# First layer of a four-layer graph kernel: records, score parts and cleared sums made inside the block that computes the scores

## The chip, the cores and the metric

One core of a Trainium2 chip runs the whole program. The metric is device time in microseconds of one execution, the median of several; three executions of the kernel before are shown. The engines are PE (TensorE), DVE (VectorE), ACT (ScalarE), POOL (GpSimd) and SP (SyncE); POOL also issues every indirect DMA of this kernel.

## What is computed

Four residual graph layers over 3125 nodes of 128 features, each behind a layer norm and a relu. Only the first matters here. It is a graph attention of four heads over 50000 edges:

```python
h = jnp.maximum(_layernorm(x, axis=-1), 0.0)
for hd in range(H):                       # H = 4
    h = inputs * W[hd]
    s_src = h @ a[hd, :D]
    s_dst = h @ a[hd, D:]
    e = jnp.exp(jax.nn.leaky_relu(s_src[src] + s_dst[dst], ALPHA))
    rowsum = jax.ops.segment_sum(e, src, num_segments=N)
    agg = jax.ops.segment_sum(e[:, None] * h[dst], src, num_segments=N)
    outs.append(jax.nn.elu(agg / rowsum[:, None]))
x = x + jnp.mean(jnp.stack(outs, axis=-1), axis=-1)
```

## The kernel before

Nodes lie in 25 blocks of 128 (NB = 25, P = 128, D = 128), so a quantity over all nodes and features is a tile of 128 partitions by 3200 elements. The program is a sequence of blocks. Inside a block each engine has its own list of instructions, ordered by semaphores; a block ends when all engines have reached its end, and only then does any engine begin the next one. Nothing is scheduled by a planner: the order of each engine is the order in which the code is written.

`first_layer` (L1854) runs these blocks in a row:

- `layer_norm_once` makes `h`. Beside it POOL runs `put_records` (L911), which writes the sorted edges into a table in HBM, one indirect DMA for 128 edges, and waits after every four until they have landed. 391 such puts are spread over three blocks.
- A short block in which SP loads the weights `w_all`, `w_col` and `a_col`.
- `scores_once` (L440) computes the two scores of each node and head, `s_col` and `d_col`, with exact error terms. ACT scales, PE transposes, ACT copies the transposed strips into `p` and `e`, and DVE sums them. At each head's end DVE raises `added`; ACT's last strip is counted in `taken`, and PE's in `turned`. POOL issues the remaining 289 puts beside it (PUT_BEFORE = 102 to ET = 391) and waits for their landing at its end (`wait_landed`).
- `store_records` (L1482) builds one record of 520 numbers (RECORD) for each node: four heads of 128 products `h * W[k]` and a one behind each, then the four scores `d`. DVE makes the products, one instruction for each head over all 25 node blocks (L1492), ACT copies the scores (L1497), POOL sets the ones (L1502). When all nine are made, POOL scatters the records to `rec_dram`, one indirect DMA for each node block, in the sorted order of the nodes (L1505), and waits for the landing of all 25.
- `spread_parts` (L1510) splits `s_col` into three bf16 parts on DVE (L1526 to L1531), transposes them on PE (L1539), and DVE copies the result to `s_rows` (L1533).
- A block in which POOL clears `y`, the sums, 128 by 12900 numbers (L1885), and the counter `passed` (L1886).
- `end_layer` frees the semaphores behind a barrier, the number of passes is read into registers, and the loop over passes begins. There is one pass here: `sum_neighbours` starts with an iota on POOL (L1618), loads 416 rows of the table, gathers 416 times 128 records (L1628), weighs them and adds them to `y` (L1702).
- `finish_once` divides and applies elu.

Of the kernel before, what the change touches and what calls it, by code (L numbers as in the profile page):

```python
# [10 lines left out]
BF16 = mybir.dt.bfloat16  # L11
# [425 lines left out]
            act.activation(root[:, :], var[:, :], ACT.Sqrt).then_inc(a, 1)  # L437


def scores_once(nc, K, h, w_col, a_col, s_col, d_col, table, listed):  # L440

# [6 lines left out]
    with ExitStack() as stack:  # L448
# [9 lines left out]
        v, turned, taken = c.sem("v"), c.sem("turned"), c.sem("taken")  # L458
        scaled, product_made, error_made, added = c.sem("scaled"), c.sem("product_made"), c.sem("error_made"), c.sem("added")
        units = [("p", 0, 0), ("p", 0, 1), ("e", 0, 0), ("e", 0, 1)]  # L460
        for k in range(1, heads):
# [8 lines left out]
        @block.gpsimd  # L470
        def _(pool):
            put_records(pool, K, table, PUT_BEFORE, ET, listed)
            wait_landed(pool, listed, ET)

        @block.tensor
        def _(pe):
            def turn(n, src, at, count):

                if n >= RING:
                    pe.wait_ge(taken, n - RING + 1)  # L480
                for b in range(count):
                    last = pe.transpose(bank[n % RING][:, b * P:(b + 1) * P], src(at + b), K["ident"][:, :])
                last.then_inc(turned, 1)

            for m in range(STRIPS):
                turn(m, lambda b: h[:, b, :], 4 * m, min(4, NB - 4 * m))
            for n, (kind, k, side) in enumerate(units):
                rows = p_rows[:, k % 2, side, :] if kind == "p" else e_rows[:, side, :]
                if kind == "p":
                    pe.wait_ge(product_made, 2 * k + side + 1)  # L490
                else:
                    pe.wait_ge(error_made, 2 * k + side + 1)
                for m in range(STRIPS):
                    turn(STRIPS * (n + 1) + m, lambda b: rows[:, b * P:(b + 1) * P], 4 * m, min(4, NB - 4 * m))

        @block.scalar
        def _(act):
# [102 lines left out]
ROUND_MAGIC = 12582912.0  # L600
TOP_DEGREE = 4000.0
RECORD = 4 * (D + 1) + 4
KEY_STEP = 4096.0
PARTS3 = 3 * NB

# [873 lines left out]
    step(dve.scalar_tensor_tensor(out, s, 1.0, m, ALU.add, ALU.mult))  # L1479


def store_records(nc, K, h, w_all, d_col, rec_dram):  # L1482
    with ExitStack() as stack:
        c = Ctx(nc, stack, "records")
        rec = c.sb("rec", [P, NB, RECORD])
        stored, made = c.gather_sem("stored"), c.sem("made")
        block = stack.enter_context(nc.Block())

        @block.vector
        def _(dve):  # L1490
            for k in range(4):
                dve.tensor_tensor(rec[:, :, k * (D + 1):k * (D + 1) + D], h, w_all[:, k, 0:D].unsqueeze(1).to_broadcast([P, NB, D]),  # L1492
                                  ALU.mult).then_inc(made, 1)

        @block.scalar
        def _(act):
            act.copy(rec[:, :, 4 * (D + 1):RECORD], d_col[:, :, :].rearrange("p k b -> p b k")).then_inc(made, 1)  # L1497

        @block.gpsimd
        def _(pool):  # L1500
            for k in range(4):
                pool.memset(rec[:, :, k * (D + 1) + D:(k + 1) * (D + 1)], 1.0).then_inc(made, 1)  # L1502
            pool.wait_ge(made, 9)
            for b in range(NB):
                pool.indirect_dma_start(rec_dram, bass.IndirectOffsetOnAxis(ap=K["order"][:, b:b + 1], axis=0),  # L1505
                                        rec[:, b, :], None).then_inc(stored, 16)
            pool.wait_ge(stored, 16 * NB)


def spread_parts(nc, K, stage, own_col, out):  # L1510


# [341 lines left out]
def first_layer(nc, K, table, listed, rec_dram, w_dram, a_dram):  # L1854
# [3 lines left out]
    with ExitStack() as stack:  # L1858
        c = Ctx(nc, stack, "first")
        passed = c.sb("passed", [P, 1])  # L1860
        s_rows = c.sb("s_rows", [PARTS3, heads, P], BF16)
        with ExitStack() as inner:
            ci = Ctx(nc, inner, "scored")
            s_col, d_col = ci.sb("s_col", [P, heads, NB]), ci.sb("d_col", [P, heads, NB])
            h = ci.sb("h", [P, NB, D])[:, :, :]
            w_all, w_col, a_col = ci.sb("w_all", [P, heads, D + 1]), ci.sb("w_col", [P, heads]), ci.sb("a_col", [P, heads, 2])
            layer_norm_once(nc, K, h, "norm0", beside=lambda pool: put_records(pool, K, table, PUT_EARLY, PUT_BEFORE, listed))
            kept = ci.sem("kept")
            with nc.Block() as block:
                @block.sync  # L1870
                def _(sp):
                    sp.dma_start(w_all[:, :, 0:D], broadcast(w_dram)).then_inc(kept, 16)
                    sp.dma_start(w_col[:, :], w_dram.rearrange("h f -> f h"), allow_slow_non_contiguous=True).then_inc(kept, 16)
                    sp.dma_start(a_col[:, :, :], a_dram.rearrange("h (t f) -> f h t", t=2), allow_slow_non_contiguous=True).then_inc(kept, 16)
                    sp.wait_ge(kept, 48)
            scores_once(nc, K, h, w_col, a_col, s_col, d_col, table, listed)
            store_records(nc, K, h, w_all, d_col, rec_dram)
            spread_parts(nc, K, "parts", s_col[:, :, :], s_rows[:, :, :])
        with ExitStack() as inner:
            ci = Ctx(nc, inner, "rounds")  # L1880
            y = ci.sb("y", [P, NB, heads, D + 1])
            with nc.Block() as block:
                @block.gpsimd
                def _(pool):
# [3 lines left out]
            n_passes = nc.values_load(K["passes"][0:1, 0:1], min_val=1, max_val=MOST_PASSES)  # L1888
            with nc.Fori(0, n_passes) as turn:
                with ExitStack() as s:  # L1890
                    sum_neighbours(nc, Ctx(nc, s, "sum"), table, rec_dram, K, s_rows, passed, y, turn)

                end_pass(nc)
            finish_once(nc, K, y)


def sort_edges(nc, K, stack, src, dst, weight, low_dram, row_dram, x_dram, table, listed):
# [1175 lines left out]
```

## Time and profile before

| | |
|---|---|
| median of three runs | 4641.7 us (4637.39 to 4642.4) |
| the profiled execution, its own time | 4645.37 us |
| its span, first to last instruction | 4643.6 us |
| busiest engine over the span | DVE, 2849.6 us, 61% |
| POOL | 1946.6 us, 42% |
| PE | 1605.0 us, 35% |
| mean granted TensorE clock | 0.64 |

No engine is busy throughout: the program is a chain of stages that have different limits, and each block's end holds back whatever comes next. The stage of this change lies between about 1005 and 1084 us of the span. Shares over the whole span say nothing about it; the timeline of that stretch does. In the timeline a row gives the start, the duration, the engine, the line of the code, the operation, and in brackets how long the engine had stood idle and what released it ("SPq L1483" is the sequencer of SP at line 1483, a block's barrier; "issue" is a pause of the engine's own).

### The profile page before, as it was taken

To read this page: it belongs to the slowest core of one execution; us is meant where nothing else is said; L and a number is where in the kernel's file an instruction comes from. 1 tells how busy PE (TensorE), PEld (TensorE's weight loads), DVE (VectorE), ACT (ScalarE), POOL (GpSimd) and SP (SyncE) were. 2 spreads that over 40 slices of the span, in tenths; PEclk is the share of its full clock that TensorE was granted. 3 is DMA by queue.
4 is the path that set the end of the run, shared out by engine and by line. 5 is a ranking of instruction groups with operands and counts; after the bars stand their busy time and mean duration, and the time that the engine had idled before them with its cause. 6 is when DMAs were issued, how large, how long until landed. Compare 5 with 4: busy or idle time off the path is not lost. (4 is left out here: it accounts for less than half of the span.)

```text
span 4643.6 us, 47312 instructions
## 1 busy us (share of the span) xinstructions
PE 1605.0 (35%) x10711; PEld 927.3 (20%) x10711; DVE 2849.6 (61%) x4818; ACT 1636.8 (35%) x4317; POOL 1946.6 (42%) x1847
## 2 busy tenths in 40 slices
PE   3170111100000000003765333142222079899989
PEld 2150111100000000001221111021111069444444
DVE  5866399872677779894554333647878767422131
ACT  1350212101556567203665434124444465010011
POOL 0046555546777730005555555157777550000000
PEclk8585555555555555555676666565555589999999
DMA  3000000005666630001222222168888545777846
GB/s 131 15 20 1 3 1 1 1 21 160 190 185 184 184 94 0 0 0 37 54 63 72 63 63 63 24 192 263 261 256 271 164 134 147 299 239 268 282 156 204
DMA packets 215387, 553.44 MB, mean 119 GB/s; under 512 B 46177, under 2 KB 112411, under 8 KB 214404
## 3 DMA queue, kind: packets, MB, share of 16 engines
q0 software_dynamic: 99984, 272.83, 21.2%
q1 hardware_dynamic: 115188, 278.18, 17.6%
q8 instruction: 82, 1.34, 0.1%
q14 instruction: 133, 1.09, 0.1%
HBM read 485.70 MB, written 65.20 MB: 119 GB/s over the span
## 5 line engine op out<-in xcount | busy, mean ns | idle before, releaser
L2712 PE MATMUL fourth_bank<-fourth_tile,fourth_z 128*128 128x512 f16 (+1 forms) x2800 | 559.8, 361 | 19.8 <-DVEq L2873 10.1
L1192 POOL DMA_INDIRECT blend_got<-rec,blend_slot x416 | 401.0, 964 | 368.6 <-DMA blend_got<-rec,blend_slot 254.8
L917 POOL DMA_INDIRECT table<-edges_record,edges_place x391 | 412.7, 1055 | 294.0 <-DMA table<-edges_record,edges_place 187.8
L2074 POOL DMA_INDIRECT heads_got<-rec,heads_slot x416 | 474.1, 1140 | 134.2 <-issue 126.4
L1628 POOL DMA_INDIRECT sum_got<-rec,sum_slot x416 | 456.5, 1097 | 142.5 <-issue 122.2
L247 PE MATMUL blend_count<-blend_mov,blend_stat 128*128 x980 | 337.9, 440 | 360.6 <-DVE blend_mov L1244 259.4
L1702 DVE TENSOR_TENSOR rounds_y<-rounds_y,sum_got 128x516 f32 x416 | 290.9, 699 | 113.3 <-DVE rounds_y L1702 29.8
L203 PE MATMUL edges_p_key<-kept_ident,edges_key_row 128*128 128x128 f32 x4 | 1.1, 428 | 1019.9 <-DVEq L170 1019.9
L2712 PEld LDWEIGHTS fourth_bank<-fourth_tile,fourth_z 128*128 128x128 f16 x2800 | 261.7, 99 | 311.7 <-issue 15.2
L1244 DVE TENSOR_SCALAR blend_mov<-built_iota_low,built_low 128x800 f16 x490 | 216.2, 442 | 170.8 <-PE blend_count L247 100.5
L2163 DVE TENSOR_TENSOR heads_got<-heads_got,heads_factor 128x390 f32<-128x390 f32 x416 | 232.1, 558 | 108.9 <-issue 99.4
L1232 DVE SCALAR_TENSOR_TENSOR second_sums<-blend_got,blend_weight,second_sums 128x129 f32 x416 | 123.7, 349 | 272.6 <-DMA blend_got<-rec,blend_slot 240.5
L2187 DVE TENSOR_TENSOR third_a_y<-third_a_y,heads_got 128x520 f32 x416 | 287.7, 692 | 1.1 <-DVE third_a_y L2187 0.2
L1719 ACT ACTIVATE sum_got<-sum_got,edges_place 128x129 f32<-128x129 f32 x672 | 197.6, 388 | 239.4 <-DVEq L1679 239.4
L2225 ACT ACTIVATE heads_got<-heads_got,heads_factor 128x65 f32<-128x65 f32 x832 | 217.4, 340 | 89.2 <-DVEq L2157 89.2
L1272 ACT ACTIVATE blend_gap<-built_iota_ten,built_offset 128x128 f32 x490 | 196.8, 402 | 125.3 <-issue 73.0
L247 PEld LDWEIGHTS blend_count<-blend_mov,blend_stat 128*128 x980 | 100.1, 102 | 604.3 <-issue 578.6
L1719 ACT ACTIVATE sum_got<-sum_got,sum_weights 128x129 f32<-128x129 f32 x576 | 169.4, 387 | 121.3 <-DVEq L1679 121.3
L203 PEld LDWEIGHTS edges_p_key<-kept_ident,edges_key_row 128*128 128x128 f32 x4 | 0.7, 216 | 1020.6 <-issue 1020.6
L247 PE MATMUL heads_degrees<-heads_one,heads_flipped 128*128 128x1 f16 x625 | 36.7, 169 | 450.1 <-ACT heads_flipped L2214 362.4
L130 POOL MEMSET edges_src_i<- 128x128 int32 x1 | 0.2, 204 | 417.8 <-POOLq L1081 417.8
L1274 ACT ACTIVATE blend_stat<-blend_gap x490 | 151.5, 309 | 54.3 <-ACT blend_gap L1272 0.8
(666 smaller groups left out, 4401.4 us busy)
## 6 DMA issues: line engine op xcount, KB each, us to landing
fourth_tile<-cs SPq DMA_DIRECT2D x100, 800.0 KB, 4.5
fourth_tile<-ct SPq DMA_DIRECT2D x100, 800.0 KB, 4.3
ct<-blend_cst SPq DMA_DIRECT2D x20, 1000.0 KB
heads_counts<-ct SPq DMA_DIRECT2D x25, 800.0 KB, 8.5
cs<-heads_flipped SPq DMA_DIRECT2D x25, 800.0 KB, 5.3
attend_cnt<-ct SPq DMA_DIRECT2D x50, 256.0 KB, 2.9
sort_low_wide<-low SPq DMA_DIRECT2D x4, 3136.0 KB
attend_cnt<-ct SPq DMA_DIRECT2D x25, 288.0 KB, 3.8
```

Source lines behind the costliest of these rows:

```text
L247: return pe.matmul(out, lhsT, rhs, start=False, stop=True, skip_group_check=True)
L917: pool.indirect_dma_start(table, bass.IndirectOffsetOnAxis(ap=K["place"][0:lanes, t:t + 1], axis=0), K["record"][0:lanes, t, :], None).the ...
L1192: pool.indirect_dma_start(got[:, buf, r, :], None, rec_dram, bass.IndirectOffsetOnAxis(ap=slot[:, t:t + 1], axis=0)).then_inc(gathered[t % ...
L1244: dve.tensor_scalar(at_slot(mov, at), K["iota_low"][:, :], K["low"][:, bass.ds(t, 1)], None, ALU.is_equal).then_inc(mov_ready, 1)
L1628: pool.indirect_dma_start(got[:, t % (HELD * PART), :], None, rec_dram, bass.IndirectOffsetOnAxis(ap=slot[:, t:t + 1], axis=0)).then_inc(g ...
L1702: dve.tensor_tensor(sums, sums, got[:, t % (HELD * PART), 0:heads * F1], ALU.add).then_inc(added, 1)
L1719: last = act.activation(part, part, ACT.Copy, scale=weights[half][:, k, r:r + 1])
L2074: pool.indirect_dma_start(got[:, buf, r, :], None, rec_dram, bass.IndirectOffsetOnAxis(ap=slot[:, t:t + 1], axis=0)).then_inc(gathered[buf ...
L2163: dve.tensor_tensor(part, part, factor[:, buf, r, ON_ACT:heads].unsqueeze(2).to_broadcast([P, heads - ON_ACT, F1]), ALU.mult).then_inc(sca ...
L2187: dve.tensor_tensor(out, out, got[:, buf, r, 0:WIDTH], ALU.add).then_inc(added, 1)
L2225: last = act.activation(part, part, ACT.Copy, scale=factor[:, buf, r, h:h + 1])
L2712: last = pe.matmul(bank[m][:, 0:w], z2[s % 2][:, k, part, :], tile[:, n % RING, at:at + w], start=(k == 0 and part == 0), stop=(k == NB - ...
```

## The change

`store_records` is removed, `spread_parts` is no longer called for the first layer, and the block that clears `y` is gone. Their work moves to the end of each engine's list in `scores_once`, whose end now serves for all of them:

- POOL: behind its last put, it waits for `taken`, sets the ones, clears `passed`, waits for `ones` and `numbered`, and then scatters the 25 node blocks, each behind a wait for its piece of the records. `wait_landed` for the puts comes behind the scatters, followed by the wait for the scatters' own landing.
- DVE: behind the last sums, it makes the records' products in five instructions of five node blocks and all four heads each (RECORD_GROUP = 5), where there were four of one head and all node blocks. `W` is read from PSUM (`w_bank`), where ACT has put it. Then come the bf16 split, the clearing of `y` (before on POOL, now on DVE), and the copy to `s_rows`.
- ACT: copies `W` to PSUM when the last errors are made, and `d_col` into the records when the last sums are made.
- PE: four bf16 transposes at the end of its list.

Memory is shared: the records lie over `p_rows` and `e_rows`, and `p` and `e` lie in `y`, which is now allocated for the whole layer; `w_bank` lies in the PSUM of `part`, the transposes write to the first bank of the ring.

```diff
@@ scores_once
-def scores_once(nc, K, h, w_col, a_col, s_col, d_col, table, listed):
+def scores_once(nc, K, h, w_all, w_col, a_col, s_col, d_col, s_rows, y, passed, table, listed, rec_dram):
...
-        part = c.ps("part", (P, 4 * 512))[:, 0:HALF]
-        p_rows, e_rows = c.sb("p_rows", [P, 2, 2, NP]), c.sb("e_rows", [P, 2, NP])
-        p, e = c.sb("p", [P, 2, NB, D]), c.sb("e", [P, 2, NB, D])
+        part_banks = c.ps("part", (P, 4 * 512))
+        part = part_banks[:, 0:HALF]
+        rows = c.sb("rows", [P, 6 * NP])
+        p_rows = rows[:, 0:4 * NP].rearrange("p (k s n) -> p k s n", k=2, s=2)
+        e_rows = rows[:, 4 * NP:6 * NP].rearrange("p (s n) -> p s n", s=2)
+        rec = rows[:, 0:NB * RECORD].rearrange("p (b f) -> p b f", f=RECORD)
+        y_flat = y[:, :, :, :].rearrange("p b k f -> p (b k f)")
+        p = y_flat[:, 0:2 * NP].rearrange("p (s b f) -> p s b f", s=2, f=D)
+        e = y_flat[:, 2 * NP:4 * NP].rearrange("p (s b f) -> p s b f", s=2, f=D)
+        split = c.sb("split", [P, heads, 3, NB], BF16)
+        ident16, own = c.sb("ident16", [P, P], BF16), c.sb("own", [P, heads, NB])
...
+        w_bank = part_banks[:, 0:heads * D].rearrange("p (k f) -> p k f", f=D)
+        s_bank = bank[0][:, :].bitcast(BF16)
...
@@ scores_once, gpsimd
             put_records(pool, K, table, PUT_BEFORE, ET, listed)
+            pool.wait_ge(taken, STRIPS * (len(units) + 1))
+            for k in range(heads):
+                pool.memset(rec[:, :, k * (D + 1) + D:(k + 1) * (D + 1)], 1.0).then_inc(ones, 1)
+            pool.memset(passed[:, :], 0.0)
+            pool.wait_ge(ones, heads)
+            pool.wait_ge(numbered, 1)
+            for b in range(NB):
+                pool.wait_ge(record_made, b // RECORD_GROUP + 1)
+                pool.indirect_dma_start(rec_dram, bass.IndirectOffsetOnAxis(ap=K["order"][:, b:b + 1], axis=0),
+                                        rec[:, b, :], None).then_inc(stored, 16)
             wait_landed(pool, listed, ET)
+            pool.wait_ge(stored, 16 * NB)
@@ scores_once, tensor
+            pe.wait_ge(parted, 1)
+            for k in range(heads):
+                last = pe.transpose(s_bank[0:PARTS3, k * P:(k + 1) * P], split[:, k, :, :].rearrange("p a b -> p (a b)"), ident16[:, :])
+            last.then_inc(spread, 1)
@@ scores_once, scalar
+            act.wait_ge(error_made, 2 * heads)
+            act.copy(w_bank, w_all[:, :, 0:D]).then_inc(scaled, 1)
+            act.wait_ge(added, 2 * heads)
+            act.copy(rec[:, :, heads * (D + 1):RECORD], d_col[:, :, :].rearrange("p k b -> p b k")).then_inc(numbered, 1)
@@ scores_once, vector
+            dve.sem_inc(added, heads)
+            dve.wait_ge(scaled, heads + 1)
+            for b in range(0, NB, RECORD_GROUP):
+                at = slice(b, b + RECORD_GROUP)
+                out = rec[:, at, 0:heads * (D + 1)].rearrange("p b (k f) -> p b k f", f=D + 1)[:, :, :, 0:D]
+                step(dve.tensor_tensor(out, h[:, at, :].unsqueeze(2).to_broadcast([P, RECORD_GROUP, heads, D]),
+                                       w_bank.unsqueeze(1).to_broadcast([P, RECORD_GROUP, heads, D]), ALU.mult))
+                dve.sem_inc(record_made, 1)
+            step(dve.tensor_copy(ident16[:, :], K["ident"][:, :]))
+            step(dve.tensor_copy(own[:, :, :], s_col[:, :, :]))
+            for k in range(3):
+                step(dve.tensor_copy(split[:, :, k, :], own[:, :, :]))
+                if k < 2:
+                    step(dve.tensor_tensor(own[:, :, :], own[:, :, :], split[:, :, k, :], ALU.subtract))
+            dve.sem_inc(parted, 1)
+            dve.memset(y_flat, 0.0)
+            dve.wait_ge(spread, 1)
+            step(dve.tensor_copy(s_rows[:, :, :], s_bank[0:PARTS3, 0:heads * P].rearrange("q (k l) -> q k l", l=P)))
...
+RECORD_GROUP = 5
...
-def store_records(nc, K, h, w_all, d_col, rec_dram):
...
@@ first_layer
+        y = c.sb("y", [P, NB, heads, D + 1])
...
-            scores_once(nc, K, h, w_col, a_col, s_col, d_col, table, listed)
-            store_records(nc, K, h, w_all, d_col, rec_dram)
-            spread_parts(nc, K, "parts", s_col[:, :, :], s_rows[:, :, :])
-        with ExitStack() as inner:
-            ci = Ctx(nc, inner, "rounds")
-            y = ci.sb("y", [P, NB, heads, D + 1])
-            with nc.Block() as block:
-                @block.gpsimd
-                def _(pool):
-                    pool.memset(y[:, :, :, :], 0.0)
-                    pool.memset(passed[:, :], 0.0)
-            end_layer(nc)
...
+            scores_once(nc, K, h, w_all, w_col, a_col, s_col, d_col, s_rows, y, passed, table, listed, rec_dram)
+        end_layer(nc)
...
```

How this moves instructions on POOL, at the end of the scores block. L917 is a put; L1505 and L493 are the scatter of the records; `rounds_y` is `y`. A wait is named by the semaphore's first use in the program, so the names in brackets tell that something is waited for, not what. Before:

```order
L917 DMA table<-edges_record,edges_place 6496256x2 x2
L448 UNCONDITIONAL_BRANCH [waits table_listed2,table_listed3,table_listed1,table_listed0]
L1499 UNCONDITIONAL_BRANCH [waits barrier_Pool_Activation_PE_DVE_SP_gather]
L1502 MEMSET records_rec 128x25 x4
L1505 DMA rec<-records_rec,edges_order 3200x520 [waits count_hot_ready]
L1505 DMA rec<-records_rec,edges_order 3200x520 x24
L1483 UNCONDITIONAL_BRANCH [waits count_v]
L1883 UNCONDITIONAL_BRANCH [waits barrier_Pool_Activation_PE_DVE_SP_gather]
L1885 MEMSET rounds_y 128x12900
L1886 MEMSET first_passed 128x1
```

With the change, where L970 is the same put, and `once_rows` is the tile that holds the records:

```order
L970 DMA table<-edges_record,edges_place 6496256x2 x2
L487 MEMSET once_rows 128x25 [waits lists_v]
L487 MEMSET once_rows 128x25 x3
L488 MEMSET first_passed 128x1
L493 DMA rec<-once_rows,edges_order 3200x520 [waits lists_spread,count_begun,lists_turned]
L493 DMA rec<-once_rows,edges_order 3200x520 [waits lists_spread] x24
L448 UNCONDITIONAL_BRANCH [waits table_listed3,table_listed2,count_hot_ready,table_listed1,table_listed0]
L69 ISA [waits barrier_Pool_Activation_PE_DVE_SP_gather]
L69 ISA
L1904 TENSOR_LOAD edges_passes [waits barrier_Pool_Activation_PE_DVE_SP_gather]
```

The memsets and the 25 scatters follow the last put without a branch to another block, each scatter has a wait, the memset of `y` has gone from POOL, and the two further blocks with it.

On DVE, in the same place. L1492 and L629 are the records' products, L1526 to L1531 and L632 to L637 the bf16 split. Before:

```order
L580 TENSOR_TENSOR scored_d_col<-once_acc 128x25 [waits lists_padded]
L448 UNCONDITIONAL_BRANCH [waits lists_padded]
L1489 UNCONDITIONAL_BRANCH [waits barrier_Pool_Activation_PE_DVE_SP_release]
L1492 TENSOR_TENSOR records_rec<-scored_h,scored_w_all 128x25x128 x4
L1483 UNCONDITIONAL_BRANCH
L1523 UNCONDITIONAL_BRANCH [waits barrier_Pool_Activation_PE_DVE_SP_release]
L1526 CAST parts_ident<-kept_ident 128x128
L1527 COPY parts_own<-scored_s_col 128x100 [waits count_wide_ready]
L1529 CAST parts_parts<-parts_own 128x4x25 [waits count_wide_ready]
L1531 TENSOR_TENSOR parts_own<-parts_own,parts_parts 128x100 [waits count_wide_ready]
L1529 CAST parts_parts<-parts_own 128x4x25 [waits count_wide_ready]
L1531 TENSOR_TENSOR parts_own<-parts_own,parts_parts 128x100 [waits count_wide_ready]
```

With the change, where `once_split` takes the place of `parts_parts` and `first_y` is `y`:

```order
L613 TENSOR_TENSOR scored_d_col<-once_acc 128x25 [waits lists_padded]
L629 TENSOR_TENSOR once_rows<-scored_h,once_part 128x5x4x128 [waits lists_padded,count_wide_ready]
L629 TENSOR_TENSOR once_rows<-scored_h,once_part 128x5x4x128 [waits lists_padded] x4
L632 CAST once_ident<-kept_ident 128x128 [waits lists_padded]
L633 COPY once_own<-scored_s_col 128x100 [waits lists_padded]
L635 CAST once_split<-once_own 128x4x25 [waits lists_padded]
L637 TENSOR_TENSOR once_own<-once_own,once_split 128x100 [waits lists_padded]
L635 CAST once_split<-once_own 128x4x25 [waits lists_padded]
L637 TENSOR_TENSOR once_own<-once_own,once_split 128x100 [waits lists_padded]
L635 CAST once_split<-once_own 128x4x25 [waits lists_padded]
L639 MEMSET first_y 128x12900 [waits lists_padded]
L641 COPY first_s_rows<-once_bank 75x512 [waits lists_saved]
```

The products now follow the last sum directly, and the memset of `y` stands on DVE, between the split and the copy to `s_rows`.

## Rows read from the trace of the kernel before

**Rows 1.** The profile's page: span, then section 1 (busy us, share, instructions of each engine).
```profile
span 4643.6 us, 47312 instructions
...
PE 1605.0 (35%) x10711; PEld 927.3 (20%) x10711; DVE 2849.6 (61%) x4818; ACT 1636.8 (35%) x4317; POOL 1946.6 (42%) x1847
```

**Rows 2.** Timeline 1005 to 1084 us: start us, us, engine line operation [idle before <-releaser].
```profile
1005.55 0.20 DVE L580 TENSOR_TENSOR scored_d_col<-once_acc 128x25 f32<-128x25 f32 x1
...
1007.09 0.97 POOL L917 DMA_INDIRECT table<-edges_record,edges_place  x1 [1.94 <-DMA table<-edges_record,edges_place]
...
1009.64 0.91 POOL L917 DMA_INDIRECT table<-edges_record,edges_place  x1 [0.30 <-issue]
...
1017.95 0.30 POOL L1502 MEMSET records_rec<- 128x25 f32 x4 [7.40 <-SPq L1483]
...
1017.97 0.37 ACT L1497 COPY records_rec<-scored_d_col 128x100 f32<-128x100 f32 x1 [88.38 <-PEq L448]
...
1017.99 13.70 DVE L1492 TENSOR_TENSOR records_rec<-scored_h,scored_w_all 128x3200 f32<-128x3200 f32 x4 [12.24 <-PEq L448]
...
1031.97 0.99 POOL L1505 DMA_INDIRECT rec<-records_rec,edges_order  x1 [13.71 <-DVE records_rec L1492]
...
1062.58 0.97 POOL L1505 DMA_INDIRECT rec<-records_rec,edges_order  x1 [0.30 <-issue]
...
1067.87 0.23 DVE L1526 CAST parts_ident<-kept_ident 128x128 bf16<-128x128 f32 x1 [36.18 <-PEq L1483]
...
1069.47 0.21 DVE L1529 CAST parts_parts<-parts_own 128x100 bf16<-128x100 f32 x1
...
1070.49 0.42 DVE L1533 COPY first_s_rows<-parts_bank 75x512 bf16<-75x512 bf16 x1 [0.81 <-PE parts_bank L1539]
...
1071.40 10.85 POOL L1885 MEMSET rounds_y<- 128x12900 f32 x1 [7.86 <-POOLq L1514]
...
1083.66 0.47 POOL L1618 IOTA sum_slot<- 128x416 int32 x1 [1.37 <-POOLq L71]
```

**Rows 3.** Lines view, POOL, 1030 to 1064 us: xcount | busy us, mean ns | idle before <-releasers.
```profile
L1505 POOL DMA_INDIRECT rec<-records_rec,edges_order x25 | 24.3, 971 | 21.0 <-DVE records_rec L1492 13.7 <-issue 7.3
```

**Rows 4.** Timeline 604 to 608 us: VectorE with one SBUF input beside POOL.
```profile
606.50 1.88 DVE L564 SCALAR_TENSOR_TENSOR once_e_rows<-once_part,once_al,once_e_rows 128x1600 f32<-128x1600 f32 x1
...
607.02 0.97 POOL L917 DMA_INDIRECT table<-edges_record,edges_place  x1 [0.30 <-issue]
```

**Rows 5.** Lines view by form, VectorE: one input in SBUF, one in PSUM; two in SBUF.
```profile
L560 DVE TENSOR_TENSOR once_part<-once_hh,once_part 128x1600 f32<-128x1600 f32 x8 | 14.6, 1829 | 0.3
...
L1492 DVE TENSOR_TENSOR records_rec<-scored_h,scored_w_all 128x3200 f32<-128x3200 f32 x4 | 13.7, 3488 | 12.2 <-PEq L448 12.2
```

**Rows 6.** Timeline 427 to 465 us (norm0): VectorE and POOL side by side.
```profile
427.75 3.49 DVE L344 TENSOR_TENSOR norm_big<-norm_big,norm_col 128x3200 f32<-128x3200 f32 x1
...
428.86 3.23 POOL L917 DMA_INDIRECT table<-edges_record,edges_place  x1 [0.30 <-issue]
...
460.60 4.36 POOL L917 DMA_INDIRECT table<-edges_record,edges_place  x1 [0.30 <-issue]
...
463.01 1.83 DVE L426 TENSOR_SCALAR scored_h<-scored_h 128x3200 f32<-128x3200 f32 x1
```

**Rows 7.** Timeline, third layer: scatters of the same kind and their block's exit.
```profile
3059.67 0.97 POOL L1953 DMA_INDIRECT rec<-third_h_rows,edges_order  x1 [0.30 <-issue]
...
3060.94 0.97 POOL L1953 DMA_INDIRECT rec<-third_h_rows,edges_order  x1 [0.30 <-issue]
...
3066.30 0.23 DVE L1526 CAST parts_ident<-kept_ident 128x128 bf16<-128x128 f32 x1 [7.59 <-PEq L1926]
```

**Rows 8.** Timeline around 510 us: exit of the norm0 block.
```profile
508.54 0.97 POOL L917 DMA_INDIRECT table<-edges_record,edges_place  x1 [0.30 <-issue]
...
514.23 0.40 SPq L1872 DMA_DIRECT2D scored_w_all<-in_L_gnn_W_dram  x1
```

**Rows 9.** Tile rounds_y: ns min/median/max, first and last start us, forms.
```profile
L1702 DVE TENSOR_TENSOR rounds_y<-rounds_y,sum_got x416: 695/697/736, 1149.3 to 1752.3; 128x516 f32 x139
```

More of the change, by code:

```diff
@@ L452, in scores_once @@
         HALF = NP // 2
-        part = c.ps("part", (P, 4 * 512))[:, 0:HALF]
-        p_rows, e_rows = c.sb("p_rows", [P, 2, 2, NP]), c.sb("e_rows", [P, 2, NP])
-        p, e = c.sb("p", [P, 2, NB, D]), c.sb("e", [P, 2, NB, D])
+        part_banks = c.ps("part", (P, 4 * 512))
[9 more added lines that the diff above has]
+        ident16, own = c.sb("ident16", [P, P], BF16), c.sb("own", [P, heads, NB])
         acc, s, t, u = (c.sb(n, [P, 2, NB, LANES])[:, :, :, :] for n in ("acc", "s", "t", "u"))
         bank = [c.ps(f"bank{k}") for k in range(RING)]
+        w_bank = part_banks[:, 0:heads * D].rearrange("p (k f) -> p k f", f=D)
+        s_bank = bank[0][:, :].bitcast(BF16)
         v, turned, taken = c.sem("v"), c.sem("turned"), c.sem("taken")
+        ones, spread, record_made, numbered, parted = (c.sem(n) for n in ("ones", "spread", "record_made", "numbered", "parted"))
+        stored = c.gather_sem("stored")
         scaled, product_made, error_made, added = c.sem("scaled"), c.sem("product_made"), c.sem("error_made"), c.sem("added")
@@ L487, in _ @@
             for n, (kind, k, side) in enumerate(units):
-                rows = p_rows[:, k % 2, side, :] if kind == "p" else e_rows[:, side, :]
+                source = p_rows[:, k % 2, side, :] if kind == "p" else e_rows[:, side, :]
                 if kind == "p":
@@ L493, in _ @@
                 for m in range(STRIPS):
-                    turn(STRIPS * (n + 1) + m, lambda b: rows[:, b * P:(b + 1) * P], 4 * m, min(4, NB - 4 * m))
+                    turn(STRIPS * (n + 1) + m, lambda b: source[:, b * P:(b + 1) * P], 4 * m, min(4, NB - 4 * m))
+            pe.wait_ge(parted, 1)
+            for k in range(heads):
+                last = pe.transpose(s_bank[0:PARTS3, k * P:(k + 1) * P], split[:, k, :, :].rearrange("p a b -> p (a b)"), ident16[:, :])
+            last.then_inc(spread, 1)
         @block.scalar
@@ L1479, in exp_once @@
     step(dve.scalar_tensor_tensor(out, s, 1.0, m, ALU.add, ALU.mult))
-def store_records(nc, K, h, w_all, d_col, rec_dram):
[L1483 to L1497, printed above, removed]
-        @block.gpsimd
-        def _(pool):
[L1501 to L1507, printed above, removed]
 def spread_parts(nc, K, stage, own_col, out):
@@ L1875, in _ @@
                     sp.wait_ge(kept, 48)
-            scores_once(nc, K, h, w_col, a_col, s_col, d_col, table, listed)
-            store_records(nc, K, h, w_all, d_col, rec_dram)
-            spread_parts(nc, K, "parts", s_col[:, :, :], s_rows[:, :, :])
-        with ExitStack() as inner:
-            ci = Ctx(nc, inner, "rounds")
-            y = ci.sb("y", [P, NB, heads, D + 1])
-            with nc.Block() as block:
-                @block.gpsimd
-                def _(pool):
-                    pool.memset(y[:, :, :, :], 0.0)
-                    pool.memset(passed[:, :], 0.0)
-            end_layer(nc)
[L1888 to L1894, printed above, removed]
+            scores_once(nc, K, h, w_all, w_col, a_col, s_col, d_col, s_rows, y, passed, table, listed, rec_dram)
+        end_layer(nc)
+        n_passes = nc.values_load(K["passes"][0:1, 0:1], min_val=1, max_val=MOST_PASSES)
+        with nc.Fori(0, n_passes) as turn:
+            with ExitStack() as s:
+                sum_neighbours(nc, Ctx(nc, s, "sum"), table, rec_dram, K, s_rows, passed, y, turn)
+            end_pass(nc)
+        finish_once(nc, K, y)
 def sort_edges(nc, K, stack, src, dst, weight, low_dram, row_dram, x_dram, table, listed):
```

## The prediction

> **What bounds the kernel now.** I began with the page. The span is 4643.6 us, and the busiest engine, DVE, works for 61% of it [rows 1], so no share names a bound; the stage that is changed has to be read by itself. The second view is the timeline from the last sums of the scores to the start of the pass [rows 2]. There one chain sets the time, and it passes from POOL to DVE and back twice:
>
> - DVE ends the last score at 1005.75, POOL issues its last put from 1009.64 to 1010.55. The scores block is thus POOL's, by 4.8 us. Then nothing starts until 1017.95, when the block has ended.
> - DVE makes products for 13.7 us, and POOL idles 13.7 us for them. The first scatter starts at 1031.97.
> - POOL issues 25 scatters, the last at 1062.58, and DVE has been idle for 36.2 us when its next block opens at 1067.87.
> - The split, four transposes and a copy end at 1070.91. POOL clears `y` from 1071.40 for 10.85 us. The pass opens at 1083.66, 1.37 us after POOL's last memset.
>
> Of the 78 us between 1005.75 and 1083.66 only the scatters, their landing and the last step into the pass have to stay; the rest waits on something that another engine could have done meanwhile. The third view is the line group of the scatters [rows 3]: 971 ns busy and 0.30 us pause each, so 30.61 us from the first start to the last (24 periods of 1.275 us).
>
> **The change, part by part, against the profiled execution.**
>
> 1. *Block end and products leave POOL's path.* Before, POOL goes from its last put (end 1010.55) to its first scatter (1031.97) in 21.42 us [rows 2]. With the change there is no block end. POOL sets the ones (four memsets, 0.30 us together) and clears `passed`; with the pauses between I put 0.85 us, so the first scatter starts at 1011.4. It needs the first piece by then. DVE is free at 1005.75, while POOL still has three puts to issue. A piece is 5 x 4 x 128 = 2560 elements. One operand lies in SBUF and one in PSUM, as in L560, where 1600 elements take 1829 ns; 3200 with both in SBUF take 3488 ns [rows 5]. The slope between them is 1.037 ns per element, so a piece takes 2.82 us, the five 14.3 us with their pauses, against 13.7 us for the four before. The first is made at 1008.7 and the last at 1020.1. POOL spends 6.4 us on the five scatters of a piece, so no later piece can be late: the split into pieces matters only through the first one. `W` in PSUM costs ACT one copy, made long before, since ACT is idle for 88.4 us ahead of L1497 [rows 2]; the copy of `d_col`, 0.37 us, starts at 1005.8 and hides under the last puts. Gain: 21.42 - 0.85 = **20.6 us**.
>
> 2. *Do the products hold up POOL?* In norm0 they would: a put beside a DVE instruction of 3.49 us with two SBUF inputs takes 3.23 us, one that also met a one-input TENSOR_SCALAR took 4.36 us and ended after it [rows 6], against 0.97 us elsewhere. In the scores block, DVE instructions of 1.88 us with one input in PSUM leave the put at 0.97 us [rows 4]. The new products are of that second kind. I take nothing for this; if they were of the first kind, see the second rival.
>
> 3. *Scatters.* The same 25, now each behind a wait. The third layer's scatters stand behind two waits each and still start 1.27 us apart [rows 7]. 0 us. The last one starts at 1011.4 + 30.6 = 1042.0, and its landing stays.
>
> 4. *The parts' block goes.* From 1067.87 to 1071.40, **3.5 us** [rows 2]. The same instructions now run on DVE from 1020.1, for some 1.9 us, under the scatters.
>
> 5. *The clearing of `y` goes from POOL.* From 1071.40 to the end of its memsets, 1.37 us before the iota: **10.9 us** [rows 2]. On DVE it is new, and no row shows a DVE memset of that size. By the two-input slope, 1.037 ns per element, 12900 elements take 13.5 us; by the fast TENSOR_SCALAR, 3200 in 1.83 us [rows 6], 7.4 us. I take 13.5, the slower. It begins at 1022.0 and ends at 1035.5; the copy to `s_rows` ends by 1036. POOL's last landing is not before 1046, so DVE has 10 us to spare. That cover is the scatters; without it all 14 us would be on the path.
>
> 6. *Block ends.* A block opened 5.29 us after the last scatter's start (1062.58 to 1067.87), landing included, and 5.36 us in the third layer [rows 7]. One plain step is 0.49 us (1070.91 to 1071.40), the step into the pass 1.37 us. The new end has the landing and the step into the pass: 5.29 - 0.49 + 1.37 = 6.2 us. So one plain step goes as well: **0.5 us**.
>
> The sum is 20.6 + 3.5 + 10.9 + 0.5 = 35.5 us, or told forward: 1042.0 + 6.2 = 1048.2 for the iota in place of 1083.66. Everything behind keeps its instructions and its order, so the profiled execution would take 4645.4 - 35.5 = 4609.9 us. That execution is 3.7 us above the median of the three runs; from the median, 4641.7 - 35.5 = **4606.2 us**, 0.76% less.
>
> Here the row and a rule of the notes meet, on the memset. The row: a one-input DVE instruction at the fast rate did hold a put [rows 6]. If the memset ran that way, POOL's issue in progress would be stretched to its end. The Trainium skill (SBUF — State Buffer, Who interferes with whom) says that a DVE instruction with at most one SBUF input, outside the modes that use both ports, does not contend with GpSimd, and (VectorE: DVE Perf Modes, Zero memsets can be issued as uint32) that a memset takes one cycle per element whatever the type. By that rule the sum stays 35.5 us; by the row it is the second rival's. No run here has shown it yet.
>
> **The rivals.**
>
> *The exit stays long.* After the last put at 1009.64 the block took 8.31 us to give way (1017.95), though a put lands within about 1.94 us of the issue's end [rows 2]. After the last scatter it took 5.29 us, with a longer transfer. The norm0 block, with 54 puts on POOL and no wait for landing at its end, also took 5.69 us from its last put's start to SP's first DMA [rows 8]. So something of some 4 us follows long lists of puts. If it belongs to the long block and not to the puts' own landing, the new exit has it too: gain 35.5 - 4 = 31.5, time 4610.2 us. The step after `y` and the short records block speak for "short blocks exit fast"; that wait_landed now comes 31 us after the puts speaks for its vanishing. The Trainium skill (Runtime: NRT & Kernel Launch, Instruction fetch mechanics) says that a taken branch out of the instruction window costs a fetch, which would side with this rival.
>
> *The memset holds POOL.* It starts at 1022.0, and one scatter is then under way until it ends. POOL loses up to 13.5 - 1 = 12.5 us, by the fast rate 6.4 us. Gain 23.0 or 29.1, time 4618.7 or 4612.6 us. If the products held it as in norm0 too, then POOL would issue about one DMA for each until 1020, some 8 more of loss: 4627 us.
>
> *The pieces run slowly.* A four-level pattern with two broadcasts has no row. If it took twice the time, the first piece is made at 1011.5, still in time; the last at 1034.4, each before POOL asks. But split and memset then end at 1050, 3 us after the landing: gain 32, time 4609.5 us. It would be hidden up to that point; so even a change that fails to speed the making of records gives most of the gain.
>
> *Slower than before.* The pass reads and adds into `y` in another place of memory, and `sum_got` moves too. Its sums are 416 instructions of 697 ns one after another [rows 9]. If each cost more, the gain is gone from 35.5 / 416 = 85 ns each, and 9.3 us slower than before from 108 ns: 4651 us. Against it: over 25 places in `y` and 32 buffers the same instruction spans only 695 to 736 ns, so the place does not matter.
>
> **How the numbers follow.** What can be told from no change is 0.2%, 9.3 us. Forecast 0.62; exit long 0.19; memset or products hold POOL 0.11; slow pieces 0.04; slower 0.01; 0.03 is left for what I have not seen, half of it within 0.2%. The likeliest is 4606.2 us. Down, the three runs of before reach 4.3 us below their median, and a step or two may be shorter than I took: low 4600. Up, the range takes in the long exit and the memset that holds POOL for its whole length, 4618.7, and ends at 4620. Faster by over 0.2% means below 4632.4: 0.97; same 0.02; slower 0.01.
>
> **What would show it.** Right: in the timeline POOL's first scatter starts within 1 us of its last put's end, the 25 scatters keep 971 ns and 0.30 us, five products of 2.8 us lie on DVE from 1005.8, one memset of 13.5 us beside scatters of unchanged length, and the iota at about 1048. Wrong: a scatter longer than 2 us; POOL waiting for a product; an idle of 8 us or more behind the last scatter; a DVE that ends after 1046; or a loss behind 1084 us, with L1702 above 700 ns.

## The result, and the profile after

The changed kernel takes 4610.1 us (median of 6 runs, 4606.79 to 4615.96) against 4640.5 us before (6 runs, 4636.79 to 4643.64). The ratio is 0.9938, with a 95% interval of 0.9925 to 0.995: 30.4 us less by the medians. The forecast was 4606.2 us with a range of 4600 to 4620. Direction and range held; of the 35.5 us that were forecast, 5 are missing.

The page of the changed kernel, span and section 1, which answers to [rows 1]:

```profile
span 4605.1 us, 47286 instructions
...
PE 1605.9 (35%) x10711; PEld 922.6 (20%) x10711; DVE 2862.2 (62%) x4820; ACT 1637.7 (36%) x4318; POOL 1927.7 (42%) x1846
```

DVE is busier by 12.6 us and POOL less busy by 18.9 us. Some 11 us of either are the clearing of `y`, which has changed its engine; POOL's other 8 us are indirect DMAs of the whole program that were a little shorter in this execution. Nothing in these shares tells of the 30 us. The timeline of the stage does; it answers to [rows 2]:

```profile
1001.51 0.20 DVE L613 TENSOR_TENSOR scored_d_col<-once_acc 128x25 f32<-128x25 f32 x1
...
1001.86 14.69 DVE L629 TENSOR_TENSOR once_rows<-scored_h,once_part 128x2560 f32<-128x2560 f32 x5
...
1003.73 0.91 POOL L970 DMA_INDIRECT table<-edges_record,edges_place  x1 [0.30 <-issue]
1004.64 0.32 POOL L487 MEMSET once_rows<- 128x25 f32 x4
1004.85 0.12 POOL L488 MEMSET first_passed<- 128x1 f32 x1
1005.54 0.99 POOL L493 DMA_INDIRECT rec<-once_rows,edges_order  x1 [0.57 <-POOL once_rows L487]
...
1021.43 10.81 DVE L639 MEMSET first_y<- 128x12900 f32 x1 [2.87 <-issue]
...
1032.16 0.36 DVE L641 COPY first_s_rows<-once_bank 75x512 bf16<-75x512 bf16 x1
...
1036.15 0.97 POOL L493 DMA_INDIRECT rec<-once_rows,edges_order  x1 [0.31 <-issue]
1048.21 0.47 POOL L1643 IOTA sum_slot<- 128x416 int32 x1 [11.09 <-POOLq L71]
```

The group of the scatters, in the lines view of POOL from 1001 to 1038 us of the changed kernel, answers to [rows 3]:

```profile
L493 POOL DMA_INDIRECT rec<-once_rows,edges_order x25 | 24.3, 971 | 7.9 <-issue 7.0 <-POOL once_rows L487 0.6 <-DVEq L631 0.3
```

Read from the last put's end, since the profiled executions differ by a few us ahead of it: the pass opened 73.1 us after it before (1010.55 to 1083.66) and opens 43.6 us after it now (1004.64 to 1048.21), 29.5 us less. The first scatter starts 0.90 us after the last put (the forecast had 0.85), the scatters keep their 971 ns, and the last one starts 30.61 us after the first, as forecast. DVE is ready at 1032.5, 3.6 us before POOL issues its last scatter. Only the last step is off: from the last scatter's start to the iota 12.06 us, where 6.2 were put. Those 5.9 us are nearly the whole difference between 29.5 and 35.5.

The sequencer's own instructions show where it lies. A drain is the instruction with which each engine ends its list of a block. These are POOL's (ns min/median/max, start). In the kernel before, at the end of the scores and at the end of the records' block:

```profile
L448 POOLq DRAIN  x1: 5682/5682/5682, 1012.0 to 1012.0; - x1
...
L1483 POOLq DRAIN  x1: 2102/2102/2102, 1065.5 to 1065.5; - x1
```

And at the end of the scores block of the changed kernel, which now has the puts and the scatters:

```profile
L448 POOLq DRAIN  x1: 7724/7724/7724, 1039.2 to 1039.2; - x1
```

The last data had landed by 1038.9. The drain runs from 1039.2 to 1046.9 while every engine and every DMA queue stands still. 5.68 + 2.10 = 7.78, within 0.06 us of 7.72: the merged block's end seems to pay both bills at once. The forecast had taken the exit of a block with 25 scatters for the exit of any block.

### The profile page after: what moved, and what is told of

Read it like the earlier page. It is cut to its first block and busy times, and to the rows that moved or that the text cites. A ratio compares the mean times of both kernels' runs of the same rounds, so it can differ in the third digit from the quotient of the medians.

```text
span 4605.1 us, 47286 instructions
## 1 busy us (share of the span) xinstructions
PE 1605.9 (35%) x10711; PEld 922.6 (20%) x10711; DVE 2862.2 (62%) x4820; ACT 1637.7 (36%) x4318; POOL 1927.7 (42%) x1846
## 5 line engine op out<-in xcount | busy, mean ns | idle before, releaser
L970 POOL DMA_INDIRECT table<-edges_record,edges_place x391 | 409.1, 1046 | 293.1 <-DMA table<-edges_record,edges_place 183.6
L1727 DVE TENSOR_TENSOR first_y<-first_y,sum_got 128x516 f32 x416 | 290.8, 699 | 115.5 <-DVE first_y L1727 28.7
L505 PE MATMUL once_bank<-kept_ident,once_rows 128*128 128x128 f32 x400 | 64.2, 337 | 341.2 <-ACT first_y L528 233.1
```

The costliest lines, as they stand in the source:

```text
L970: pool.indirect_dma_start(table, bass.IndirectOffsetOnAxis(ap=K["place"][0:lanes, t:t + 1], axis=0), K["record"][0:lanes, t, :], None).the ...
L1727: dve.tensor_tensor(sums, sums, got[:, t % (HELD * PART), 0:heads * F1], ALU.add).then_inc(added, 1)
```

## The experiments

Theory A: each indirect DMA leaves work to the next drain, so that the 5.68 us of the puts were only moved. Theory B: the long exit belongs to the block's long list and its branch. The runs fall in three sessions on two chips, in which the kernel before takes 4639.85, 4651.88 and 4745.53 us. So totals are compared by their ratio, and stages within the profile by spans of time: from the last score (end of `scored_d_col`) to the iota, 46.5 us in the changed kernel, 77.9 before. (By this measure the stage has won 31.4 us and not 29.5, since the last put also ended nearer to the last score: 2.9 us behind it in place of 4.8.)

**A drain behind the puts.** Edit to the changed kernel:

```diff
             put_records(pool, K, table, PUT_BEFORE, ET, listed)
+            pool.drain()
             pool.wait_ge(taken, STRIPS * (len(units) + 1))
```

> The changed kernel with one more drain on POOL, straight behind its last put of the scores block. In the changed kernel the drain at that block's end takes 7.72 us after 289 puts and 25 scatters; before, two drains took 5.68 us (289 puts) and 2.10 us (25 scatters). Theory A (each indirect DMA since the last drain leaves POOL some work, which its next drain does): the new drain takes 5.5 to 7 us, landing included, the drain at the block's end falls from 7.72 to about 2.1 us; the total is the same or up to 1.5 us more, 4610 to 4612 us. Theory B (the long exit belongs to the length of the block's list and the branch at its end): the new drain is short, under 1.5 us, the one at the end stays at 7 to 8 us, total 4610 to 4612 us.

Measured: 4612.58 us, ratio 0.9943 (0.9926 to 0.9961). The new drain (L485) and the one at the block's end (L448) in this run:

```profile
L485 POOLq DRAIN  x1: 8389/8389/8389, 1005.3 to 1005.3; - x1
...
L448 POOLq DRAIN  x1: 2096/2096/2096, 1048.3 to 1048.3; - x1
```

The first began to count while two puts were still to be issued; the last put ends at 1008.00 and this drain at 1013.7, so 5.7 us are its own, with the landing of the last puts inside them. The one at the end fell from 7.72 to 2.10 us, and the last scatter's start to the iota from 12.06 to 6.44 us, 0.3 from the forecast's 6.2. Next to nothing is won between last score and iota (45.7 us, and 43.7 from the last put's end, where the changed kernel has 43.6), since the same time is paid earlier. Theory A holds in so far as the time belongs to the indirect DMAs and goes to the first drain behind them. B falls: the list and the branch are as they were, and the exit is short.

**The records in one piece.** `RECORD_GROUP = 25` in place of 5.

> The records made in one instruction of 25 node blocks in place of five of 5. Theory (the first piece is all that the pieces buy): one DVE instruction of 12800 elements, about 13.4 us; POOL's first scatter starts 13.5 to 14 us after the last score in place of 4.0, so 9.5 to 10 us later, and all behind it too: 4620 us. Rival (POOL is not waiting for the pieces at all, since its puts end late enough): no change, 4610 us.

The timeline of this run:

```profile
1005.20 13.49 DVE L629 TENSOR_TENSOR once_rows<-scored_h,once_part 128x12800 f32<-128x12800 f32 x1
...
1019.55 0.99 POOL L493 DMA_INDIRECT rec<-once_rows,edges_order  x1 [11.24 <-DVEq L631]
...
1062.21 0.47 POOL L1643 IOTA sum_slot<- 128x416 int32 x1 [11.09 <-POOLq L71]
```

POOL stood 11.24 us for the one product. Last score to iota took 57.2 us, 10.7 more than with five pieces. The ratio, 0.9972 (0.9962 to 0.9982; 4628.59 us), is worse by another 5 us or so: in the profiled execution the second layer's loop took 12.6 us longer than in the changed kernel's (from its iota to the third layer's). It did so in later runs with other edits too and was at 924 us before, so I take that for its own variation; it is not shown.

**`W` from SBUF.** In the products, `w_all[:, :, 0:D].unsqueeze(1)` in place of `w_bank.unsqueeze(1)`.

> The products read W from SBUF, so both inputs lie in SBUF; the copy to PSUM stays. Theory (two SBUF inputs hold an indirect DMA of POOL until the DVE instruction ends, as in the norm0 block): puts and scatters beside the five products take 2 to 3 us each in place of 0.97; over 14 us POOL issues 4 to 6 in place of 10, and loses 5 to 8 us: 4615 to 4618 us. Rival (no contention): scatters stay at 0.97 us, 4610 us.

The timeline of this run, where five products fill 1007.23 to 1021.9:

```profile
1007.23 14.71 DVE L629 TENSOR_TENSOR once_rows<-scored_h,scored_w_all 128x2560 f32<-128x2560 f32 x5
1008.12 2.72 POOL L970 DMA_INDIRECT table<-edges_record,edges_place  x1 [0.30 <-issue]
...
1011.43 2.46 POOL L493 DMA_INDIRECT rec<-once_rows,edges_order  x1 [0.27 <-POOL once_rows L487]
1014.20 2.64 POOL L493 DMA_INDIRECT rec<-once_rows,edges_order  x1 [0.30 <-issue]
1017.14 2.67 POOL L493 DMA_INDIRECT rec<-once_rows,edges_order  x1 [0.30 <-issue]
1020.12 2.67 POOL L493 DMA_INDIRECT rec<-once_rows,edges_order  x1 [0.30 <-issue]
...
1023.09 0.97 POOL L493 DMA_INDIRECT rec<-once_rows,edges_order  x1 [0.30 <-issue]
```

One indirect DMA for each product, as in norm0 [rows 6]; behind the last product the next takes 0.97 us again. The products themselves keep their 2.82 us. Last score to iota 53.6 us, 7.1 more; 4618.49 us, ratio 0.9955 (0.9938 to 0.9972). So the operand in PSUM, which looks like a detail of the diff, is worth 7 us between last score and iota.

**`y` cleared by POOL**, in the same block, behind the last scatter (`pool.memset(y_flat, 0.0)` in place of DVE's).

> The clearing of y goes back to POOL, behind its last scatter. Theory (clearing on DVE is fully hidden, on POOL only the landing of 1.8 us hides in it): the pass opens 9 us later, 4619 us. If the drain of 7.7 us also ran beside the clearing: the pass opens 1.3 to 3 us later, 4612 us. Rival (clearing on DVE cost POOL something through the shared port): less than 9 us, with scatters shorter than in the changed kernel.

The timeline of this run:

```profile
1041.29 0.97 POOL L493 DMA_INDIRECT rec<-once_rows,edges_order  x1 [0.30 <-issue]
1042.26 10.87 POOL L495 MEMSET first_y<- 128x12900 f32 x1
...
1062.20 0.47 POOL L1643 IOTA sum_slot<- 128x416 int32 x1 [9.07 <-POOLq L71]
```

Last score to iota 55.4 us, 8.9 more; 4619.5 us, ratio 0.996 (0.9948 to 0.9971). Only the landing hid in the clearing. The drain did not: it ran its 7.7 us behind the memset. And the scatters are 971 ns long with DVE's memset beside them and without it, so that memset does not hold POOL.

**Waits for landing after every 8 puts.** In the scores block alone:

```diff
-            put_records(pool, K, table, PUT_BEFORE, ET, listed)
+            put_records(pool, K, table, PUT_BEFORE, ET, listed, 8)
...
-def put_records(pool, K, table, first, end, listed):
+def put_records(pool, K, table, first, end, listed, held=IN_FLIGHT):
...
-        if t % IN_FLIGHT == 0 and t:
+        if t % held == 0 and t:
```

> The changed kernel, but in the scores block POOL waits for the landing of its puts after every 8 in place of every 4. Of the 72 waits of 1.94 us, half go, some 59 us, so POOL ends its puts long before DVE ends the scores, and the first scatter waits for the first piece of records (2.8 us after the last score, 4.0 before). From the last score to the opening of the pass: 46.5 us in the changed kernel, 45.6 to 46 expected; the drain at the block's end stays near 7.7 us, since the same 289 puts and 25 scatters stand ahead of it. Total 4609 us. If the drain's length came from how closely the puts follow each other, it would be longer.

The same with a drain behind it:

```diff
-            put_records(pool, K, table, PUT_BEFORE, ET, listed)
+            put_records(pool, K, table, PUT_BEFORE, ET, listed, 8)
+            wait_landed(pool, listed, ET)
+            pool.drain()
```

> As the run before, and POOL drains behind its puts, while it would wait for the records anyway. Theory A (the drain pays for what the puts have left): the new drain takes 5 to 8 us and costs nothing, the drain at the end falls to 2.1 us, from the last score to the opening of the pass 40 to 40.5 us, 6 us less than in the changed kernel: 4604 us. Rival (the drain's work is not saved up but repeated, or the scatters suffer): 45 us or more, 4609 us.

POOL ended its puts at 947.8 and 947.6 us, 63 us ahead of the last score. Without the drain, the block's end took 7.73 us and last score to iota 47.0 us: no gain, although POOL had been idle for 63 us. Idle time alone does not pay the debt. With the drain in that idle time (L486), the one at the end (L448) is short:

```profile
L486 POOLq DRAIN  x1: 5682/5682/5682, 949.0 to 949.0; - x1
...
L448 POOLq DRAIN  x1: 2176/2176/2176, 1048.2 to 1048.2; - x1
```

Last score to iota 41.3 us, 5.7 less than without it. In the total it can't be told: 4628.24 us, ratio 0.995 (0.9934 to 0.9967), and 4627.05 us, ratio 0.9946 (0.9929 to 0.9962), against 0.9938 (0.9925 to 0.995) of the changed kernel. The scores themselves took 490.9 us in both, against 487.5 in the changed kernel, and DVE's instructions in them sum to 439.8 and 440.0 us against 437.1. So some 3 of the 5.7 us are given back there, perhaps because DVE and POOL meet more often; that is not shown. I had also put the first scatter 2.8 us behind the last score; it came after 3.8, as in the changed kernel, since the first piece ends 2.97 us after the last score and POOL begins 0.9 later. In the changed kernel, then, the first scatter waits for the first piece too. DVE signals that piece at 1004.72, while POOL's last put ends at 1004.64; the scatter follows the signal by the same 0.8 us as in these runs. Where the piece was long made, as in the run with a drain at put 300 below, the scatter comes 0.59 us after the last put and not 0.90:

```profile
1017.74 0.32 POOL L489 MEMSET once_rows<- 128x25 f32 x4
1017.96 0.11 POOL L490 MEMSET first_passed<- 128x1 f32 x1
1018.33 0.99 POOL L495 DMA_INDIRECT rec<-once_rows,edges_order  x1 [0.27 <-POOL once_rows L489]
```

**`y` cleared in two halves** on DVE.

> The clearing of y on DVE in two instructions of 6450 elements. In the changed kernel the one of 12900 is on record with 10.81 us, behind an unexplained 2.87 us. If a memset really takes 1.04 ns per element and its record begins late by a fifth of it, each half has a pause of about 1.4 us and 5.4 us, and the sum is again 13.5 to 13.7 us. If the pause is a wait of its own (for the port that POOL uses, for the split), the first half has 2.9 us and the second none. Total unchanged, 4610 us, since it is hidden.

The timeline of DVE in this run (one execution, 4622.81 us):

```profile
1025.67 5.43 DVE L639 MEMSET first_y<- 128x6450 f32 x1 [1.52 <-issue]
1032.40 5.43 DVE L640 MEMSET first_y<- 128x6450 f32 x1 [1.29 <-issue]
1037.75 0.36 DVE L642 COPY first_s_rows<-once_bank 75x512 bf16<-75x512 bf16 x1
```

Both halves have their pause, and it goes with their size, so it is no wait for a port or for the split: the record of this memset begins late by about a fifth of the whole. Pause and record together are 13.7 us for 12900 elements in both runs, 1.06 ns each with the instruction's fixed part. The forecast's 13.5 us is near it, and the row's 10.81 is not all of the engine's time.

**A drain in the middle of the puts**, at number 300.

> The changed kernel with a drain on POOL in the middle of its puts, behind number 299; 91 puts and 25 scatters follow until the block's end, 116 in place of 314. If each indirect DMA since the last drain costs the next one 84 ns (2.10 us for 25), without a limit below 116, the drain at the end takes 9.7 us, more than the 7.72 us after 314: something must free part of the debt on the way in the longer row. If the debt simply grows slowly with the number, it is shorter than 7.7 us, about 4 us. Total 4610 to 4620 us, with the new drain's own time on POOL's path.

The drain in the middle (L485) and the one at the end (L448) of this run:

```profile
L485 POOLq DRAIN  x1: 10854/10854/10854, 852.7 to 852.7; - x1
...
L448 POOLq DRAIN  x1: 2341/2341/2341, 1051.9 to 1051.9; - x1
```

This was a miss. 91 puts and 25 scatters behind a drain leave 2.34 us, neither 9.7 nor 4. So 84 ns for each DMA fits only 25 scatters (2.10 us); 289 puts leave 5.68, 314 DMAs leave 7.72, and 116 leave 2.34. Some of the debt is freed on the way, and I can't say by what rule. Total 4622.27 us, ratio 0.9938 (0.9921 to 0.9956). Last score to iota took 47.0 us, although the drain in the middle had put the last put off to 9.1 us behind the last score: from that put's end the pass opened in 37.9 us, against 43.6 in the changed kernel.

**A better version, and both kernels again.** Waits after every 8 puts only for the last 87, then the landing and a drain:

```diff
-            put_records(pool, K, table, PUT_BEFORE, ET, listed)
+            put_records(pool, K, table, PUT_BEFORE, 304, listed)
+            put_records(pool, K, table, 304, ET, listed, 8)
+            wait_landed(pool, listed, ET)
+            pool.drain()
```

> As with a wait after every 8 puts and a drain behind them, but only the last 87 puts wait every 8, so that POOL is ready, drained, just before DVE ends the scores, and the two engines compete less on the way. Theory A: the drain at the block's end is 2.1 to 2.2 us, from the last score to the opening of the pass 41 us (46.5 in the changed kernel), the scores themselves 488 us as in the changed kernel and not 491 us. Total 5 to 6 us below the changed kernel on the same chip. Rival: the gain in the stage is real but something behind it gives it back, total equal to the changed kernel.

> The changed kernel once more, on the same chip as the run above, as its measure. Last score to the opening of the pass 46.5 us, drain at the block's end 7.7 us; the pass, 675.1 us against 672.4 us before in one profile each: if that is noise of one execution, this and the next run lie between without order; if it belongs to the change, this one is near 675 and the next near 672.

> The kernel before once more, for a second profile. Last score to the opening of the pass 78 us, drains 5.7 and 2.1 us. The pass near 672 us if the difference belongs to the change, anywhere from 672 to 677 us if it is noise.

| | last score to iota | drain at the scores' end | the pass | total | ratio to before |
|---|---|---|---|---|---|
| late waits and a drain | 40.9 us | 2.09 us | 689.2 us | 4723.34 us | 0.9954 (0.9936 to 0.9971) |
| changed kernel again | 46.5 us | 7.72 us | 689.2 us | 4722.73 us | 0.9961 (0.9948 to 0.9974) |
| before again | 74.8 us | 5.68 us | 688.8 us | 4743.62 us | 0.9997 (0.998 to 1.0014) |

This chip is slower by some 2% in all three. Of the 107 us between the two profiles of the kernel before, about 16 lie in each of the first two layers behind their iotas and 65 behind the third layer's. The stage does what was expected, 5.6 us less than in the changed kernel, but the total does not show it: the scores took 494.6 us in that profile against 487.4. Of these 7.2 us, 4.7 are one wait of DVE for ACT's strips (16.95 against 12.25 us), which I have no cause for, and about 2 are longer DVE instructions. The runs of these two kernels spread over 14 and 18 us here, those of the kernel before over 34. Whether this version beats the changed kernel is open.

The pass took 689.2 and 688.8 us in this pair, where the first two profiles had 675.1 and 672.4. That speaks for noise, but does not settle it: from the iota to the end of the last addition into `y`, the one profile of before in the earlier sessions has 669.4 us, and all nine of the changed kernel and its variants there have 670.8 to 673.4. A loss of 1 to 4 us in the pass is not excluded.

The changed kernel's own gain came out smaller here: ratio 0.9961 and 22.8 us by the medians (4745.53 to 4722.73), against 0.9938 and 30.4 us at first. In the stage the gain is the same: from the last put's end to the iota 43.6 us against 73.1, as in the first two profiles. Where the other 7 us went is not shown.

## Why the prediction was right or wrong

1. *Block end and products leave POOL's path: right in size, with some luck.* First scatter 0.90 us behind the last put; pieces of 2.82 us, as worked out. But the forecast had the first piece ready 2.7 us before POOL needs it, and there was no margin: the last put ended 2.9 us behind the last score and not 4.8, and the piece was signalled 0.08 us after it. POOL's own step is 0.59 us, not 0.85; the other 0.3 us are a wait for the piece, and the two errors cancel. The five take 14.69 us with their pauses, 0.4 more than I put, without effect. That only the first piece matters is shown by the one-piece run, +10.7 us.
2. *The products do not hold POOL: right,* and shown from the other side by the run with `W` in SBUF, +7.1 us.
3. *Scatters: right,* 971 ns and 30.61 us, waits and all.
4. *and 5. The parts' block and the clearing: right.* Both are off the path; DVE is done at 1032.5. The clearing put back on POOL costs 8.9 us rather than 10.9, since the landing hides in it. The second rival, a memset that holds POOL, fell: no scatter beside it is longer. The Trainium skill's rule that a DVE instruction with at most one SBUF input does not contend with GpSimd (SBUF — State Buffer, Who interferes with whom) agrees with the changed kernel's trace, where no scatter beside products or memset is longer than 0.99 us. Its one cycle per element for a memset whatever the type (VectorE: DVE Perf Modes, Zero memsets can be issued as uint32) fits too: 13.7 us of pause and record are 1.06 ns per element, near the 1.037 ns of the forecast's slope.
6. *Block ends: wrong.* The step was "5.29 - 0.49 + 1.37 = 6.2 us" for the new end. It took an exit after 25 scatters for an exit after 289 puts and 25 scatters. It is 12.06 us, and of the 5.9 us between, 5.6 are POOL's drain, 7.72 in place of 2.10, and 0.3 are further steps. The row for it was in hand: [rows 2] shows 8.31 us from the last put to the next block, and the first rival named it, at 4 us and with a chance of 0.19. It should have been the forecast, since nothing in the change removed whatever caused it. The norm0 exit that this rival also cited [rows 8] is a drain of POOL as well: it ends at 513.99, 4.5 us behind the end of that block's last put, and SP's first DMA follows at 514.23. With 5.9 in place of nothing the sum is 29.6 us, and 4641.7 - 29.6 = 4612 us against the measured 4610.1. The rival's cause was open between the puts and the block; the drain run decides for the puts. The Trainium skill's rule that a taken branch out of the instruction window costs a fetch (Runtime: NRT & Kernel Launch, Instruction fetch mechanics) has no part in these 5.6 us: the drain run has the same branch and a short exit.

The slower rival fell as well: L1702 of before is L1727 here with the same 697 ns. In the rival of slow pieces, a gain of 32 us makes 4609.7 us and not 4609.5.

## What to carry to other kernels

When blocks are merged, sum up what each of them paid at its own end: work that its transfers have left to be done is not saved by removing the barrier that collected it, only moved to the next one. Look for it in the sequencers' rows of a line, where a drain of several us stands though no engine and no queue shows work. Where DVE works beside indirect DMAs, try to give it one operand from PSUM: for these products that choice was worth 7 us, nearly a quarter of the gain. And pieces are worth what the first one brings forward; later ones are free as soon as the consumer is slower than the producer. Here the first scatter still waits for the first piece, so a smaller first one might bring it forward a little; no run tried it.

## What was not expected of the hardware

- POOL's drain costs 5.68 us after 289 indirect DMAs that have all landed, 2.10 us after 25 (2.09 to 2.11 at three later block ends of the kernel before), 7.72 us after both, and 2.34 us after 91 and 25. 63 us of idle in between do not shorten it (7.73 us), and it is not covered by a memset of POOL that stands ahead of it.
- The record of a DVE memset of 12900 elements is 10.81 us long and begins 2.87 us after the engine is free; two halves have 5.43 us each, behind 1.52 and 1.29 us. The sum, 13.7 us both times, is what the memset costs.
- The second layer's loop took from 919.7 to 940.3 us over these profiles: 919.7 to 932.9 in the earlier sessions, 935.4 to 940.3 on the last chip, and in both pairs 2 to 4 us longer before than with the change. A gain of 5 us in one stage can be read from that stage's rows, and not from a total.
